# The mask of the fourth pair of heads ahead of the split of k on GpSimd, in an attention stage on one Trainium2 core

## The reference

```
Q, K = normalize(x @ W_q.T), normalize(x @ W_k.T);  V = x @ W_v.T
Qn = normalize(Q @ W_nudge)                      # per head, 4 x 4
scores = Qn @ K * SCALE + k_bonus(K)             # the bonus depends on the key alone
attn = softmax(where(causal, -inf, scores));  out = (attn @ V) @ W_out.T
x = x + layernorm(out)
```

## Time and profile before

| | before |
|---|---|
| median of 3 runs | 1826.87 us (1824.72 to 1830.86) |
| the profiled execution | 1828.17 us, span 1826.4 us |
| mean granted clock of TensorE | 0.969 |
| PE busy | 1664.5 us, 91% |
| DVE busy | 1356.9 us, 74% |
| POOL busy | 990.9 us, 54% |
| ACT busy | 890.1 us, 49% |
| the 26 looped rounds of the attention | 632.56 us, from 110.55 to 743.11 |

### The profile page before, as it was taken

The page is one execution under the profiler, slowest core; times in us unless marked ns, Lnnn a source line. Parts: engine busy times, 40 slices in busy tenths (PEclk is TensorE's granted clock), DMA queues, the critical chain, the costliest instruction groups (busy, mean ns, idle before and its releaser), DMA issues.

```text
span 1826.4 us, 43279 instructions
## 1 busy us (share of the span) xinstructions
PE 1664.5 (91%) x12768; PEld 1245.9 (68%) x12768; DVE 1356.9 (74%) x4113; ACT 890.1 (49%) x2003; POOL 990.9 (54%) x1779
## 2 busy tenths in 40 slices
PE   3999999999999999975999999999999998669996
PEld 2676666676776666754778888888888886435553
DVE  6788888888888887764466777777777775648886
ACT  2665656665556665532444444444444443224443
POOL 5777777777777777752222333333333333227777
PEclk8999999999999999997999999999999999579998
DMA  1011111111111111201011000000000002434441
GB/s 41 10 38 42 52 52 52 52 52 52 44 34 52 52 52 52 81 13 41 12 58 58 30 30 30 30 29 29 29 29 29 29 24 88 155 105 134 130 134 44
DMA packets 78239, 95.76 MB, mean 52 GB/s; under 512 B 7046, under 2 KB 62995, under 8 KB 78160
## 3 DMA queue, kind: packets, MB, share of 16 engines
q1 hardware_dynamic: 70992, 77.91, 13.6%
q0 software_dynamic: 7168, 16.87, 2.6%
HBM read 53.14 MB, written 43.69 MB: 53 GB/s over the span
## 4 chain that ended last, share of the span: by engine, by line
PE 46%; DVE 3%; issue 2%; POOL 2%; ACT 1%; DMA 0%; DVEq 0%; POOLq 0%; SPq 0%; ACTq 0%
PE main L1243 7%; PE main L1245 6%; PE main L1252 6%; PE main L1431 4%; PE main L1269 3%; PE yp L1402 3%; PE xi L1219 3%; PE main L1386 2%; PE main L1389 2%; PE main L1387 2%; PE main L1290 2%; PE route L1445 1%; PE turn L1212 1%; PE xi L1445 1%; PE yp L1453 1%
## 5 line engine op out<-in xcount | busy, mean ns | idle before, releaser
L653 ACT ACTIVATE wgu<-score 128x384 f32<-128x384 f32 x512 | 223.2, 489 | 103.1 <-PE score L476 101.7
L498 PE MATMUL outp<-wgu 128*64 128x256 f32 (+1 forms) x2048 | 197.9, 336 | 29.8 <-POOL wgu L321 28.7
L321 POOL TENSOR_SCALAR_AFFINE_SELECT wgu<-wgu 128x512 f32<-128x512 f32 x256 | 167.1, 653 | 104.4 <-ACT wgu L653 92.1
L1243 PE MATMUL main<-hT_high,h_high 128*128 128x512 f32 x512 | 221.2, 432 | 0.9 <-ACT hT_high L1503 0.9
L1245 PE MATMUL main<-hT_high,h_low 128*128 128x512 f32 x512 | 201.3, 393 | 0.0
L498 PEld LDWEIGHTS outp<-wgu 128*64 128x64 f32 x2048 | 129.4, 138 | 89.5 <-issue 36.4
L1252 PE MATMUL main<-hT_low,h_high 128*128 128x512 f32 x512 | 138.4, 391 | 0.1
L792 DVE TENSOR_TENSOR wgu<-spread,wgu 128x512 f32<-128x512 f32 x128 | 88.5, 691 | 61.0 <-PE spread L520 46.3
L1843 DVE SCALAR_TENSOR_TENSOR th<-th,main 128x512 f32<-128x512 f32 x64 | 43.9, 686 | 114.0 <-ACT th L1570 114.0
L534 PE MATMUL back<-wout,wgu 128*128 128x128 f32 x1024 | 128.1, 279 | 0.0
L1219 PEld LDWEIGHTS xi<-state,wh_sb 128*128 128x128 f32 x512 | 93.8, 196 | 41.0 <-ACT state L1480 23.9
(11 more groups left out here) (272 smaller groups left out, 4299.7 us busy)
## 6 DMA issues: line engine op xcount, KB each, us to landing
sorted_d<-row_buf SPq DMA_DIRECT2D x26, 772.0 KB, 3.7
xg<-sorted_d SPq DMA_DIRECT2D x48, 386.0 KB, 3.1
wgu<-in_gate_up SPq DMA_DIRECT2D x4, 2048.0 KB, 9.4
xa<-in_x SPq DMA_DIRECT2D x32, 128.0 KB, 3.5
xr<-in_x SPq DMA_DIRECT2D x32, 128.0 KB, 3.2
x_d<-x SPq DMA_DIRECT2D x32, 128.0 KB, 1.9
x1c<-x_d SPq DMA_DIRECT2D x16, 256.0 KB, 2.8
x1v<-x_d SPq DMA_DIRECT2D x16, 256.0 KB, 2.8
```

Source lines behind the costliest of these rows:

```text
L321: pool.affine_select(out=blocks, in_=blocks, compare_op=ALU.is_ge, fill=0.0, base=0, pattern=[[0, 4], [1, P]], channel_multiplier=-1).then ...
L498: m = pe.matmul(outp[DV * i:DV * (i + 1), p % 2, k * P:T], val[par][:, k, h, :], weights(h, k), start=(k == 0), stop=(k == 1), tile_positi ...
L653: act.activation(prob[:, h // 2 % (RING // 2), :, h % 2, :], score[h % BANKS][:, 0:SC].rearrange("p (c q) -> p c q", q=P), ACT.Exp).then_i ...
L1243: pe.matmul(main[m % 2][:, :], w[0][:, k, m * P:(m + 1) * P], src[0][:, k, :], start=(k == 0), stop=False)
```

## The change

In a round that prepares a next sequence, POOL masks pair 3 right behind pair 2, ahead of the split of k, where the mask stood between the split of k and the copies to k_aug. No operation, size or semaphore is changed; the last piece of the split is now followed by the wait for the split itself.

```diff
                     bonus(f, lambda p: mask(b, p))
+                    mask(b, 3)
                     wait_apart(pool, s["kcopy"], f + 1, s["const"])
                     wait_apart(pool, s["p_kaT"], f, s["const"])
                     split(k5, k_part, "ksplit", f)
-                    mask(b, 3)
                     wait_apart(pool, s["ksplit"], STEPS_K * (f + 1), s["const"])
```

## The result

The changed kernel takes 1797.3 us (median of 4 runs, 1794.97 to 1799.34), against 1827.48 us for the one before (4 runs, 1824.72 to 1830.86): a ratio of 0.9833, with a 95% interval of 0.9821 to 0.9844, 30 us faster. The forecast was 1800.5 us with a range of 1796 to 1811. In a later session the same kernel took 1797.23 us (median of 5 runs) against 1827.99 (9 runs), a ratio of 0.9837 [0.9822, 0.9853].

What follows compares the result with a forecast made beforehand. PE's own order sets 23.28 us a looped round, its waits for POOL's mask the rest. Removing 25.6 us in the loop and 0.8 in b = 30, 26.4 in all, takes 1826.87 to 1800.5 us; range 1796 to 1811.

Steps and rivals of the forecast that it cites:

- What bounds the kernel: In the 26 looped rounds PE's own order sets 23.28 us a round; its waits for POOL's mask set the rest.
- PE's wait removed, 25.6 us in the loop: PE's wait before L498 on the fourth pair's mask goes entirely, 25.6 us over the 26 looped rounds.
- The wait of b = 30: Behind the loop, PE's wait on the mask in round b = 30 goes too, 0.8 us.
- The clock, 0 to 1.6 us: A low-clock piece at 704 to 708, behind one stall, might go: 0 to 1.6 us of further gain.
- The split of k at no cost: POOL's k_aug ends at +13.9 us of the round, PE turns it at +15.46: hidden, 1.5 us to spare.
- the split of q at no cost: On POOL, masks 4 and 5 end at +15.2 us, split of q starts at +15.40: covered by 0.2, priced at 0.
- The 0.09 us at the reciprocal: DVE's reciprocal L778 ends 0.09 us before PE's L506 wants it; delay beyond 0.3 us in all lands on PE.
- DVE at no cost: DVE's L792 has 0.23 us to spare before PE's L520; cost 0 to 0.41 us a round, taken as 0.
- The level: Total gain of 26.4 us for the whole kernel, giving 1800.5 us.
- B: Part given back by DVE's L792 or POOL's q split and reciprocal, 0.1 to 0.4 us a round; chance 0.18.
- D: The stall only moves: k_aug or q_aug comes as late for PE; 1822 to 1832 us; chance 0.03.
- E: Slower: the mask holds POOL for head 7's exponential with both splits behind it; 1833 us; chance 0.02.

Runs made afterwards that it cites:

- moving the mask by doses: Fourth pair's mask placed inside the split of k, after four or two of its five operations: 26 looped rounds 616.77 or 603.75 us, against 632.56 before the change.
- the padded kernels: Changed kernel plus a POOL memset of 128 x 512 or 128 x 1024 elements between fourth pair's mask and split of k: loop 605.78 or 620.68 us.
- the longer memset: Changed kernel plus a POOL memset of 128 x 1024 elements (0.95 us) ahead of the split of k: loop 620.68 us, run 1817.78.
- the fifth mask: Changed kernel with the fifth pair's mask also moved ahead of the split of k: loop 667.90 us, run 1869.79.
- scores_first: Changed kernel with PE's scores of the third pair ahead of projection L584: loop 602.75 us, run 1797.50.
- the two followers: Changed kernel, third pair's scores ahead of L584, plus POOL's second-pair mask one operation earlier and DVE's reciprocal L778 ahead of q4: 1791.03 us.
- the mask after four operations: Fourth pair's mask placed inside the split of k after four of its five operations, against the changed kernel's mask ahead: loop 616.77 us, run 1810.29.

## Why the prediction was right, point by point

**What bounds the kernel.** Right. The loop fell by 28.8 us of the span's 28.8, and moving the mask by doses moved the loop with it. That the 23.28 us a round agreed with the 23.29 of b = 2 was luck: b = 2 waits 0.22 us at L584 and a looped round 0.16, and this hid the error of 0.06 us that comes next. Without the stall a looped round takes 23.22 us, and b = 2 still took 23.28 in the kernel after.

**PE's wait removed, 25.6 us in the loop.** Right, with one small error of reading. The earlier trace rows give 1.31 us of idle before L498, counted from the modelled end of the scores at 314.99. Without a wait L498 does not start at that end but 0.27 us after the start of the scores, overlapping their last 0.07 us (305.65 and 305.92 above). Each stall therefore costs about 0.06 us more than its idle: the round is 23.22 us and not 23.28, 1.6 us over 26 rounds.

**The wait of b = 30.** 0.8 us was forecast; rounds 29 and 30 fell from 46.66 to 45.87. The mask was late there for another reason than in the loop. It started as early as in b = 2, at +9.9 us, but took 1.07 us and not 0.64, begun 0.1 us behind DVE's running maximum in the kernel before:

```profile
776.34 0.74 DVE L841 TENSOR_TENSOR_SCAN cmax<-bonT 16x256 f32<-16x256 f32 x1
776.44 1.07 POOL L321 TENSOR_SCALAR_AFFINE_SELECT wgu<-wgu 128x512 f32<-128x512 f32 x1
```

**The clock, 0 to 1.6 us.** It came at its upper end. Round b = 27 of the kernel before had taken 26.21 us against its neighbours' 24.53 to 24.6, and no looped round after has such a piece. Only one execution of the kernel before was profiled, so how often such a piece comes is not known. So 25.6 + 1.6 + 1.6 is the loop's 28.8.

**The split of k at no cost, the split of q at no cost.** Right: their times were as forecast within 0.1 us, and the padded kernels show that the cover was real but thin: the longer memset lost all but 0.3 us of its 0.95. The 0.09 us at the reciprocal, read in one even round, was taken for both kinds, and is 0.40 in odd rounds.

**DVE at no cost.** Right; the slack of 0.23 us was too small a reading. In the even rounds the running maximum now ends earlier, at +13.50 and not at +13.76 us, since the mask that stretched L753 in the earlier trace rows is no longer beside it; in odd round b = 11 it ends later, at +13.52 and not at +13.14, with an L753 of 0.58 us beside the mask where the kernel before had one of 0.25. PE's L520 wants the L792 behind it at +14.63, and it ends at +14.24 in both, so neither is paid. Over the loop DVE's busy time fell from 516.21 to 514.05 us and POOL's rose from 467.74 to 473.44, so the harm was exchanged and not gone.

By the rule of the Trainium skill (SBUF — State Buffer, "Who interferes with whom") up to 0.64 us of DVE a round could have been lost. The trace agrees that a step is held up in the new place too: L753 takes 0.56 us beside the mask at 327.25, and 0.23 without it. None of it reached PE.

**The level.** 26.4 us was forecast and 28.8 came in the profiled execution, 30.2 between the medians. In the profiled executions the 2.4 us are 1.6 for the overlap and 1.6 for the clock, less 0.8 by which the front and the rest happened to be longer; the 1.4 us between that and the medians lie within the spread of the runs.

**The rivals.** B, D and E did not happen here, but the runs produced each: the longer pad B's late reciprocal, the fifth mask D's late k_aug and E's hold on POOL, the first at its forecast price, the second at 667.90 us where 650 to 666 was expected.

## What to carry to other kernels

Where one in-order engine serves several others, put what a consumer wants first ahead of work whose own consumer is late, and write down for each item behind it the time it ends and the time it is wanted: here 1.2, 1.5, 0.2 and 0.09 us told in advance that one mask could move and a second could not. Read each slack in every kind of round: the 0.09 was 0.40 in the other one. The bound on how early it may go is the arrival of its own input, since an instruction that waits holds the whole queue. When a consumer's wait is gone, the next one is often a few tenths away on several engines at once: scores_first alone won 1.0 us, with the two followers moved as well 6.6.

## What the runs showed of the hardware that was not expected

A semaphore wait between two dependent operations cost POOL more inside the loop than in the written-out rounds. In the loop the value waited for is in a register. In the kernel before, L334 starts 0.16 us after the end of L330 in the loop, and 0.09 us after it in round 29:

```profile
312.88 0.32 POOL L330 TENSOR_SCALAR k_part<-k 128x160 bf16<-128x160 f32 x1
313.36 0.53 POOL L334 TENSOR_TENSOR rest<-k,k_part 128x160 f32<-128x160 f32 x1
...
750.82 0.32 POOL L330 TENSOR_SCALAR k_part<-k 128x160 bf16<-128x160 f32 x1
751.23 0.58 POOL L334 TENSOR_TENSOR rest<-k,k_part 128x160 f32<-128x160 f32 x1
```

Between mask 0 and the old place of mask 3 stand 13 such steps, so this is about 0.9 us, and it fits that the written-out rounds 0, 1, 2 and 29 had no listed stall while all the looped ones had (b = 30, also written out, had one from the longer mask shown above). That it is the register was not tried apart.

TensorE's granted clock fell in looped rounds of two kernels, each time behind a stall of PE. In the kernel before, with waits of 0.7 and 1.3 us in turn, it was one round in 26. With the fifth mask ahead too, where waits of 1.2 to 1.6 us at L559 stand beside up to 0.6 at L507, it was five, each 1.5 to 1.6 us longer than others of its kind. In the first of them L559 started at 234.28 after a wait of 1.57 us; behind it the granted clock was 0.50, the 1.2 GHz level, and 0.91 as the mean of 20 us, with the rest at 1.00:

```profile
235.00:237.00 2.00, 2.00 (x17) 1.12 (x17) 0.77 (x2) 1.24 (x5) 1.48 (x4) 0.50 0.00 0
...
230.00:250.00 20.00, 18.27 (x180) 13.52 (x176) 14.74 (x41) 10.50 (x25) 15.33 (x35) 0.91 0.18 59
```

With waits of 0.8 us or less (the mask after four operations, both pads) no looped round shows it. Most rounds with the long waits kept their clock, so what decides it is not shown. In the kernel before the 1.6 us were lost for good, as the round behind took its usual 23.98. With the fifth mask four of the five slow rounds gave 0.8 to 1.0 us back in the next, where L507 did not wait for the reciprocal. So a stall here can cost a little more than its length, and one that is removed can give a little more back.
